# Routed tokens stored once per pair of keeping experts, as doubled rows, instead of once per expert

## What is computed

```python
topv, topi = jax.lax.top_k(xf @ Wg + bg, 2)
wts = softmax(topv)
order = argsort(-wts[:, 0])              # tokens by priority
xo, ti, wo = xf[order], topi[order], wts[order]
cap = int(1.25 * T / 8)                  # 15680
pos = cumulative count of each expert over ti.reshape(-1)
keep = pos < cap                         # an expert keeps its first cap picks
slot = where(keep, ti * cap + pos, drop)
y = gelu(eb @ W1 + b1) @ W2 + b2         # per expert, on its kept tokens eb
moe_o = sum over both picks of y[slot] * where(keep, wo, 0)
out1 = input + x_skip + layer_scale * moe (put back in token order)
out = silu(bn(conv3x3(attention(out1))))
```

## Time and profile before

| what | value |
|---|---|
| median of 3 runs | 5972.66 us |
| span of the profiled execution | 6004.2 us |
| conv_norm_phase | 0 to 1109 us |
| route_phase | 1109 to 1582 us |
| expert_phase | 1582 to 3835 us |
| output_phase | 3835 to 6004 us |

### The profile page before, as it was taken

The page is one execution under the profiler, slowest core; times in us unless marked ns, Lnnn a source line. Parts: engine busy times, 40 slices in busy tenths (PEclk is TensorE's granted clock), DMA queues, the critical chain, the costliest instruction groups (busy, mean ns, idle before and its releaser), DMA issues. The chain is left out here.

```text
span 6004.2 us, 66408 instructions
## 1 busy us (share of the span) xinstructions
PE 4869.7 (81%) x20680; PEld 2721.7 (45%) x20680; DVE 2405.2 (40%) x4770; ACT 1512.5 (25%) x3688; POOL 3488.9 (58%) x3508
## 2 busy tenths in 40 slices
PE   8999999310399997998779878558888888888888
PEld 3555658310255554544445444224444444444444
DVE  0012226896022222222222222356656556556553
ACT  2233336350033332333223323101111111111111
POOL 0000000004777777877777777477777777777773
PEclk9999999655599998999889989779999999999999
DMA  8887779863333333333223322323333322222310
GB/s 168 185 182 196 194 180 248 260 205 112 96 117 118 118 113 96 94 88 98 84 83 90 93 83 75 118 93 102 105 104 103 107 92 85 82 88 86 101 61 33
DMA packets 840398, 711.26 MB, mean 118 GB/s; under 512 B 596072, under 2 KB 681710, under 8 KB 836090
## 3 DMA queue, kind: packets, MB, share of 16 engines
q1 hardware_dynamic: 666362, 466.30, 28.6%
q0 software_dynamic: 109312, 139.69, 8.5%
q10 hardware_dynamic: 64512, 102.79, 5.0%
HBM read 440.11 MB, written 385.75 MB: 138 GB/s over the span
## 5 line engine op out<-in xcount | busy, mean ns | idle before, releaser
L1117 POOL DMA_INDIRECT y_ring<-ye,index_o x1568 | 1580.7, 1008 | 462.2 <-issue 460.3
L435 POOL DMA_INDIRECT xe<-chunk,slots x1568 | 1536.4, 980 | 476.8 <-issue 476.8
L1150 PE MATMUL cp<-padded,taps_o 128*128 128x448 f32 x4032 | 1627.3, 561 | 62.4 <-DVE padded L1338 62.4
L1150 PEld LDWEIGHTS cp<-padded,taps_o 128*128 128x128 f32 x4032 | 782.1, 198 | 811.8 <-issue 777.6
L921 ACT ACTIVATE hid<-hid_ps,b_cols 128x448 f32<-128x448 f32 x1120 | 709.3, 633 | 1489.6 <-PE hid_ps L875 1391.3
L883 PE MATMUL y_ps<-hid,w_sb 128*128 128x448 f32 x2240 | 932.7, 561 | 0.4 <-DVE yt L946 0.4
L875 PE MATMUL hid_ps<-xt,w_sb 128*128 128x448 f32 x2240 | 890.9, 541 | 1.5 <-DVE xt L940 1.5
L513 POOL MEMSET zeros<- 98x512 f32 x1 | 0.5, 524 | 1109.2 <-POOLq L107 1109.2
L1216 ACT ACTIVATE outb<-cp,shift,s 128x448 f32<-128x448 f32 x224 | 162.1, 724 | 1757.7 <-PE cp L1150 1757.6
L883 PEld LDWEIGHTS y_ps<-hid,w_sb 128*128 128x128 f32 x2240 | 423.1, 199 | 336.4 <-issue 335.8
L1293 DVE SCALAR_TENSOR_TENSOR logits<-y_ring,gates,logits 128x128 f32<-128x128 f32 x1568 | 432.6, 345 | 353.9 <-DMA y_ring<-ye,index_o 336.9
(11 more groups left out here) (198 smaller groups left out, 3627.4 us busy)
## 6 DMA issues: line engine op xcount, KB each, us to landing
xe<-zeros SPq DMA_DIRECT2D x16, 3920.0 KB
rows_in<-xe SPq DMA_DIRECT2D x280, 224.0 KB, 2.7
ye<-rows_out SPq DMA_DIRECT2D x280, 224.0 KB, 2.3
xin<-in_x_dram SPq DMA_DIRECT2D x256, 196.0 KB
conv<-rows ACTq DMA_DIRECT2D x256, 196.0 KB
pix<-conv SPq DMA_DIRECT2D x224, 224.0 KB, 5.1
xn<-hat SPq DMA_DIRECT2D x112, 448.0 KB, 4.3
chunk<-xn POOLq DMA_DIRECT2D x112, 448.0 KB, 3.7
```

The source lines that it names most:

```text
L435: pool.indirect_dma_start(out=self.xe[:, :], out_offset=bass.IndirectOffsetOnAxis(ap=self.slots[:, c, n * CHK + j:n * CHK + j + 1], axis=0 ...
L1117: pool.indirect_dma_start(out=y[ch][c][:, j * C:(j + 1) * C], out_offset=None, in_=ye[:, :], in_offset=bass.IndirectOffsetOnAxis(ap=index[ ...
L1150: last = pe.matmul(cp[i % 2][:, 0:HB * W], taps[:, t, :], padded[b][:, img, hb * HB + kh:hb * HB + kh + HB, kw:kw + W], start=(t == 0), st ...
```

## The change

A token is now stored once, in a class given by which experts keep it: 36 classes (8 single experts and 28 pairs) and one for tokens that nobody keeps. Each class begins at a block of 128 rows, and one DRAM tensor `xy` holds rows of 1024 bytes: the token twice. The lower expert of the pair reads the left half of a row and writes its result there, the higher expert does the same with the right half. So 7 indirect DMAs of a chunk scatter, and 7 gather, each with 128 rows of 1024 bytes. A chunk is doubled on its way in, by two plain loads of `xn` (L418 twice). `lull` is gone, and the ring of chunks has 3 buffers in place of 7.

An expert's tokens now lie in blocks of many classes, so `route_phase` also computes a table `where` of block addresses (132 positions x 8 experts, for reading and for writing), and `chunks`, how many chunks each tile needs. The expert loop has 33 tiles of an expert: 32 of four blocks (512 tokens) and a last one of two. SP now issues four loads and four stores for a tile, each at an address that it first reads with `value_load`. Instead of zeroing all rows, the kernel zeroes the blocks at both ends (3 DMAs) and the last block of each of 36 classes (18 DMAs from SP and 18 from ACT).

```diff
-EARLY_PAIRS = 2
 EARLY = 8
-LULL = 3000
+CLASSES = E * (E + 1) // 2
+TILES = 33
+POSITIONS = TILES * BLOCKS
...
 class Scatter:
-    RING = 7
+    RING = 3
...
+        rows = self.xn[g * 128:(g + 1) * 128, ch * CHK * C:(ch + 1) * CHK * C].rearrange("p (k c) -> p k c", c=C)
+        for h in range(2):
+            pool.dma_start(self.twice[i][:, :, h, :], rows).then_inc(self.chunk_in[i], 16)
...
         for j in range(CHK):
-            for c in range(2):
-                pool.indirect_dma_start(
...
+            at = j * self.chunks + n
+            pool.indirect_dma_start(
+                out=self.xy[:, :], out_offset=bass.IndirectOffsetOnAxis(ap=self.slots[:, at:at + 1], axis=0),
+                in_=self.twice[i][:, j, :, :].rearrange("p h c -> p (h c)"), in_offset=None,
+                bounds_check=limit, oob_is_err=False).then_inc(self.scattered[i], 16)
         if n:
             self.landed(pool, n - 1)
+            if n + self.RING - 1 < self.chunks:
+                self.load(pool, n + self.RING - 1)
...
+        def clear_tails(eng, c0, c1):
+            for c in range(c0, c1):
+                at = eng.value_load(tails_u[0:1, c:c + 1], min_val=0, max_val=ROWS - 128)
+                eng.dma_start(xy[bass.ds(at, 128), :], zeros[:]).then_inc(zeroed, 16)
...
+            pool.wait_ge(zeroed, 48 + 16 * CLASSES)
             pool.wait_ge(early_set, 1)
...
+            codes = [2 ** a + (2 ** b if b > a else 0) for a in range(E) for b in range(a, E)] + [0]
+            for c0, c1 in SUM_GROUPS:
+                for c in range(c0, c1):
+                    last = dve.tensor_scalar(flags[:, c], code, float(codes[c]), None, ALU.is_equal)
+                last.then_inc(flags_set, 1)
+            def place_classes(bank, before, c0, c1, g0, g1):
+                G = g1 - g0
+                ranks = bank[:, 0:(c1 - c0) * G].rearrange("p (c g) -> p c g", g=G)
+                do(dve.tensor_tensor(ranks, ranks, before, ALU.add))
+                for c in range(c0, c1):
+                    do(dve.copy_predicated(place[:, :, g0:g1], flags[:, c, :, g0:g1].bitcast(U16),
+                                           ranks[:, c - c0, :].unsqueeze(1).to_broadcast([128, CHK, G])))
...
         def _(pool):
             set_identity(pool, ident[:], ident_set)
...
                 scatter.put(pool, n, limit)
-                if n > EARLY:
-                    pool.wait_ge(rested, n - EARLY)
-                pool.memset(lull[:], 0.0).then_inc(rested, 1)
...
+                at = [sp.value_load(tables.where[0:1, bass.ds(q * BLOCKS + k, 1), 0, e:e + 1].rearrange("p q e -> p (q e)"),
+                                    min_val=0, max_val=2 * ROWS - 256 + 1) for k in range(blocks)]
+                sp.wait_ge(chunks_scattered, sp.value_load(tables.chunks[0:1, bass.ds(q, 1), e:e + 1].rearrange("p q e -> p (q e)"),
                                                            min_val=1, max_val=PR * NCHK))
-                sp.dma_start(rows_in[i][0:TM, :, :], xe[bass.ds(e * CAP + q * NT, NT), :]
-                             .rearrange("(p k) c -> p k c", k=BLOCKS)).then_inc(tile_in[i], 16)
+                for k in range(blocks):
+                    sp.dma_start(rows_in[i][:, k, :], halves[bass.ds(at[k], 256), :].rearrange("(p h) c -> p h c", h=2)[:, 0, :]
+                                 ).then_inc(tile_in[i], 16)
...
                 sp.wait_ge(out_ready, t + 1)
-                sp.dma_start(ye[bass.ds(e * CAP + q * NT, NT), :].rearrange("(p k) c -> p k c", k=BLOCKS),
-                             rows_out[i][0:TM, :, :]).then_inc(tile_out[i], 16)
+                for k in range(blocks):
+                    at = sp.value_load(tables.where[0:1, bass.ds(q * BLOCKS + k, 1), 1, e:e + 1].rearrange("p q e -> p (q e)"),
+                                       min_val=0, max_val=2 * ROWS - 256 + 1)
+                    sp.dma_start(halves[bass.ds(at, 256), :].rearrange("(p h) c -> p h c", h=2)[:, 0, :], rows_out[i][:, k, :]
+                                 ).then_inc(tile_out[i], 16)
...
-                    if first:
-                        pool.memset(y_ring[:, ch * 2 * CC:(ch + 1) * 2 * CC], 0.0).then_inc(cleared, 1)
-                        pool.wait_ge(cleared, ch + 1)
                     for j in range(CHK):
-                        for c in range(2):
-                            pool.indirect_dma_start(
...
+                        pool.indirect_dma_start(
+                            out=y[ch][:, j, :, :].rearrange("p h c -> p (h c)"), out_offset=None, in_=xy[:, :],
+                            in_offset=bass.IndirectOffsetOnAxis(ap=index[ch][:, j:j + 1], axis=0),
+                            bounds_check=limit, oob_is_err=False).then_inc(y_in[ch], 16)
```

More of the change, by code:

```diff
@@ L8 @@
 U32 = mybir.dt.uint32
+I32 = mybir.dt.int32
+U16 = mybir.dt.uint16
 ALU = mybir.AluOpType
@@ L469, in route_phase @@
[L469 to L475, removed]
-        before, rows_, tot, base = (flat_logits[:, at + i * E * GR:at + (i + 1) * E * GR] for i in range(4))
@@ new lines, in route_phase @@
+        slots_k = slots[:].rearrange("p (k g) -> p k g", k=CHK)
+        first, rel = (sb(n, [128, J]) for n in ("first", "rel"))
+        place = first[:].rearrange("p (k g) -> p k g", k=CHK)
+        same, inner = (rel[:].bitcast(BF16)[:, i * J:(i + 1) * J].rearrange("p (k g) -> p k g", k=CHK) for i in range(2))
+        ones, ones_b = sb("ones_r", [128, 128]), sb("ones_b", [128, 128], BF16)
+        below_b = sb("below_b", [128, 128], BF16)
+        bound, low, cand, count, hit, need, minus_mid, enough, weight = (
+            sb(n, [128, E]) for n in ("bound", "low", "cand", "count", "hit", "need", "minus_mid", "enough", "weight"))
@@ L542, in _ @@
             act.wait_ge(exp_ask, 1)
[L543 to L547 removed]
+            act.activation(top[1], top[1], ACT.Exp).then_inc(exp_done, 1)
             for r in range(SEARCH_STEPS):
@@ L580, in _ @@
+            last.then_inc(table_summed, 1)
+            for i in range(len(low_bank), NRG):
+                class_ranks(i)
         @block.vector
@@ L651, in _ @@
             last.then_inc(above_counted, 1)
+            prio_k, pick0_k, junk_k = by_chunk(prio), by_chunk(pick[0]), by_chunk(junk[:])
+            dve.wait_ge(ramps_set, 1)
+            dve.memset(tab, 0.0)
+            dve.memset(inner[:, 0, :], 0.0)
+            dve.memset(place, 0.0)
+            do(dve.memset(ahead[:, :, 0, :], 0.0))
+            for e in range(E):
+                last = dve.tensor_scalar(tie[:, e], prio_k[:, e], bound[:, e:e + 1], 2.0 ** e, ALU.is_equal, ALU.mult)
+            last.then_inc(ties_set, 1)
@@ new lines, in rank_within, with set_slots @@
+            def rank_within(g0, g1):
+                for d in range(1, CHK):
+                    out = inner[:, 1:, g0:g1] if d == 1 else same[:, 0:CHK - d, g0:g1]
+                    do(dve.tensor_tensor(out, code[:, d:, g0:g1], code[:, 0:CHK - d, g0:g1], ALU.is_equal))
+                    if d > 1:
+                        do(dve.tensor_tensor(inner[:, d:, g0:g1], inner[:, d:, g0:g1], same[:, 0:CHK - d, g0:g1], ALU.add))
+            def set_slots(g0, g1):
+                do(dve.tensor_tensor(slots_k[:, :, g0:g1], place[:, :, g0:g1], inner[:, :, g0:g1], ALU.add))
@@ L973, in output_phase @@
-def output_phase(nc, s, x, xn, ye, ln_beta, slots, gates, logits, out, p):
+            scale(end - 1, E - 1, False, LAST * 128)
+            result(end - 2, E - 2, TILES - 1, False, LAST)
+            result(end - 1, E - 1, TILES - 1, False, LAST)
+def output_phase(nc, s, x, xn, xy, ln_beta, slots, gates, logits, out, p):
     PR, N = s["PR"], s["N"]
```

679 lines of the change are left out of this document (434 added, 245 removed).

## The result

The changed kernel takes 7178.8 us (median of 4 runs, 7175.5 to 7179.6) where the kernel before took 5966.8 us on the same chip: a ratio of 1.202, 95% interval 1.198 to 1.206. It is 20% slower. The forecast was 5945 us, and its range ended at 6170.

A forecast was written before the change was run, and what follows sets the result against it. POOL's indirect DMAs were taken to set the end from 1418 us on. Routing -82, expert +407 and output -356 gave -31 on 6004.2, so 5973 us profiled and 5945 us for the median, range 5650 to 6170.

The forecast's parts named there:

- the part on PE: Expert stage: PE needs 7.8 us a full tile, and POOL's scatter at 11 us a chunk holds nothing up.
- SP's queue as the bound: Expert stage: SP's loads, stores and register loads take 10.1 us a tile, above PE's 7.8; stage +407 us; chance 0.67.
- a term of 0.25: Expert stage, SP's tile sum: 0.25 us of the 10.1 for semaphore arithmetic and the loop's branch.
- Register loads in a row: Expert stage, SP's queue: nine register loads a tile, each taken at 0.65 us, without overlap.
- The rival of 5695 us: Expert stage: four register loads in a row overlap, tile 9.1 us, -252 us; chance 0.13.
- the one that SP is no bound: Expert stage: SP's loads so cheap that PE's 7.8 us a tile decides, -580 us, 5365 us; chance 0.04.
- The output stage: Output stage: PE late next at 109.6 us a pair, POOL at 64; 1813 us against 2169, -356 us.
- The rival of 6080 us: POOL's indirect DMAs, early chunks and output stage: cost goes by bytes, 0.98 becomes 1.96 + 0.3 us, +135 us; chance 0.07.
- Routing: Routing stage: first slots' scatter from about 1406 us, stage ends at 1500 in place of 1582, -82 us.
- The clock rival: Expert loop: PE's idle gaps bring half clock, PE's tile 11.2 us, +277 us, 6220 us; chance 0.09.

The follow-up runs named there:

- e1_right: Changed kernel with each expert's blocks moved to the end of its positions: 6725 us, ratio 0.988 to the kernel before on the chip of 6824.
- e2_right_singles: e1_right plus each expert's single class placed behind its pair classes: 6433 us, ratio 0.944 to the kernel before on the same chip.
- e3_lull: Changed kernel with POOL's pause put back behind each of 104 chunks scattered in the expert stage: 7533 us, ratio 1.106 to the kernel before.
- e4_act3: Changed kernel with ACT issuing three of a tile's four stores, three tiles later, in place of SP: 6549 us, ratio 0.962 to the kernel before.

## Why the prediction was wrong, point by point

**The step that failed** is the sentence on POOL in the part on PE: at 11 us a chunk POOL "holds nothing up", because "a round of eight tiles takes 81 us ... and uses 112/33 = 3.4 chunks". That divides the chunks evenly over the rounds. The loop waits for what each tile's entry in `chunks` says, in the order of the queue, and one entry of 112 in round 0 stops SP until the scatter's end. Neither the even routing nor the same order as before was given by any row; I priced `where` and `chunks` as work of DVE and SP, and not as the order that they set. The price was 1102.6 us of stalls, as long as 92% of the miss of 1201 us. e1_right, e2_right_singles and e3_lull show it from three sides. No rival covered it: each changed the price of some operation or the clock, and none asked when a tile's last token arrives. The kernel before held a hint in code, the `spare` that keeps the tiles of small experts to the end, and the change has nothing in its place.

**SP's queue as the bound** was right, 5% too small. A tile in the loop takes 10.69 us where I took 10.1, just under the upper bound of 10.7 to 10.8 from the row of a store and the next load. The tile across the branch takes 13.19 us and the other seven 10.33 on average, so 0.36 of the 0.59 is the branch, which I had in a term of 0.25 with the semaphores' arithmetic, and 0.23 lies in the loads and stores themselves. 240 tiles by 0.59 are 142 us. Against that stand 20 us that the forecast has SP wait for the first result (1542 to 1562), which the stall swallowed, and 10 us that I can't assign: 1103 + 142 - 20 - 10 = 1215 us.

**Register loads in a row** do not overlap: between the end of a group of stores (3574.03 + 3.92) and the next group of loads (3581.80) lie 3.85 us, with five register loads and the arithmetic of two waits, and the four TENSOR_LOADs of the addresses in it start 0.67 us apart (3578.5 to 3580.5), each behind the assertion of the one before. The Trainium skill (DMA: Bandwidth & Descriptors, "Latency and other measured facts") puts the floor of a `tensor_load` at about 600 ns. With the arithmetic behind it (0.67 us from one to the next) that agrees, though the TENSOR_LOAD itself has a median of 266 ns. The Trainium skill says in the same place that the compiler unrolls by four to amortize that floor. Here four in a row cost as much each as one alone. The rival of 5695 us is out. So is the one that SP is no bound (e4_act3).

**The output stage** was right in its bound: 1806 us for 1813, PE waiting for sums only 27.5 us (5 times) where it waited 308, POOL idle half the time. That it came within 7 us is in part luck: a half of a pair takes 54.0 us for 54.8 (24 us less over 31), and the fifth chunk's transposes come 72 us behind the stage's start for 63, with more small waits before the first bank. **An indirect DMA of 128 rows costs the same with twice the bytes**: 991 in place of 980 ns and 1010 in place of 1008. The rival of 6080 us is out. (No run varies the number of rows.)

**Routing** was right: first scatter at 1400.3 us for 1406, end 1492 for 1500; the predicated copy that no row had shown took 930 ns for 693 elements where I took 900, and 285 for 91 where I took 270.

**The clock rival** had its mechanism and not its size. In the loop PE idles 1.8 us a tile on average (420 of 2490 us from 2700 to 5190 us, 234 tiles) at a granted clock of 0.90, and a piece of eight records behind a gap of 2.17 us takes 5.30 us, in place of 3.60 behind a gap of 0.67:

```profile
5172.49 0.66 PE L1103 MATMUL xt_ps<-ident_e,rows_in 128*128 128x128 f32 x4 [2.17 <-DMA rows_in<-xy]
5172.99 5.30 PE L1119 MATMUL y_ps<-hid,w_sb 128*128 128x512 f32 x8
...
5182.83 0.66 PE L1103 MATMUL xt_ps<-ident_e,rows_in 128*128 128x128 f32 x4 [0.67 <-DMA rows_in<-xy]
5183.32 3.60 PE L1119 MATMUL y_ps<-hid,w_sb 128*128 128x512 f32 x8
```

That is time out of PE's slack, not out of SP's 10.7 us.

The chances were 0.60 for faster or same. With the stalls taken off whole, an estimate and not a run, the time would be 7174 - 1103 = 6071 us on the first chip, inside the range and 1% above the kernel before's profiled 6004: even then the change in this form would hardly have paid there, because of SP's queue. The nearest runs give back less and are on slower chips: e2_right_singles, without the stalls, takes 6433 us on the chip of 6824, 838 us under the changed kernel's 7271 on the chip of 6656, since its tiles beside the scatter take 13.7 us. On that chip its ratio is 0.944, so there it did pay.

## What to carry to other kernels

Where an engine takes its waits from a table, read or work out the table's values from real data, first entries first, before calling the producer hidden: mean rates say nothing about an in-order queue, and one late entry at its head costs the whole overlap. When a data layout is replaced, look for what the old one did silently for the order of readiness (here the empty tiles in front). And when one large transfer becomes four at computed addresses, count the queue's register loads, and spread them over two queues from the start.

## What was not expected of the hardware

**Chips differ while POOL issues DMAs.** The kernel before takes 5967 and 5979 us in two groups of runs (perhaps on one chip), and 6656 and 6824 us on two other chips. An indirect gather has a median of 997 ns on both the first chip and the one of 6656. The register assertions of SP (ns min/median/max) are, first on one and then on the other:

```profile
L823 SPq SEQ_ASSERT  x180: 18/18/18, 2252.0 to 3748.2; - x180
```

```profile
L823 SPq SEQ_ASSERT  x161: 2/18/710, 2253.8 to 3760.0; - x161
```

and among the groups of waits on the latter stand:

```profile
ACT outb L1216 <- remote: 928.7, 61, 39.3
DVE xt L940 <- remote: 697.4, 94, 11.7
```

An instruction that takes 18 ns each of 180 times on the one takes 2 to 710 ns on the other (a minimum of 2 can also mean that the record's time stamps come late), and ACT and DVE wait hundreds of microseconds for releases that the profile can't place (remote) and that it doesn't have on the first. In these traces it is so beside POOL's scatters and gathers only: the loop of the changed kernel behind its scatter runs alike on both (gathers start at 5368.6 and 5368.9 us), and its output stage is 1900 us in place of 1806. So the kernel with half as many indirect DMAs loses 1.3% on such a chip, where the kernel before loses 11.5%, and the ratio of the two is 1.09 in place of 1.20. The cause is not shown; the trace of the kernel before on the slower chip is of a single run, whose 6730 us lie above the median of 6656 there.

**Where SP's loop branches, it loses 2.6 to 2.9 us** (13.2 us across it, against 10.6 at most and 10.3 on average between other tiles), once for eight tiles here. What of it is the branch itself, no run takes apart.
